# Moving the end of one stage and the start of the next: the slot maximum, the first logits loads and the last tile's activation

## The reference, cut to what matters

```python
logits = jnp.einsum('bnd,esd->bnes', x, phi)
dispatch = jax.nn.softmax(logits, axis=1)                      # over the nodes
combine = jax.nn.softmax(logits.reshape(B, N, E * S), axis=-1) # over all 4096 slots
slots = jnp.einsum('bnd,bnes->besd', x, dispatch)
h = jax.nn.gelu(jnp.einsum('besd,edh->besh', slots, w1) + b1[None, :, None, :])
y = jnp.einsum('besh,ehd->besd', h, w2) + b2[None, :, None, :]
out = jnp.einsum('besd,bnes->bnd', y, combine)
```

## Time and profile before

| what | us |
|---|---|
| median of three runs | 1797.23 (1797.04 to 1797.39) |
| the profiled execution's own time | 1797.73 |
| its span, first to last instruction | 1795.9 |
| mean granted clock of TensorE, share of full | 0.972 |
| TensorE busy in the span | 1620.2 |
| VectorE busy | 1103.3 |
| ScalarE busy | 848.6 |

### The profile page before, as it was taken

The page is one execution under the profiler, slowest core; times in us unless marked ns, Lnnn a source line. Parts: engine busy times, 40 slices in busy tenths (PEclk is TensorE's granted clock), DMA queues, the critical chain, the costliest instruction groups (busy, mean ns, idle before and its releaser), DMA issues. The chain is left out here.

```text
span 1795.9 us, 27185 instructions
## 1 busy us (share of the span) xinstructions
PE 1620.2 (90%) x9543; PEld 952.1 (53%) x9543; DVE 1103.3 (61%) x1844; ACT 848.6 (47%) x1306; POOL 267.8 (15%) x123
## 2 busy tenths in 40 slices
PE   6886664899999899899998999999999959998998
PEld 3433332565665566455544666655556536665555
DVE  7999997799999554532222555555555555665301
ACT  2269997888888454211112333333333335555100
POOL 0000001788788141000000000000000000000000
PEclk9999988799999999999999999999999989999999
DMA  4001000012222320311102211222222134441111
GB/s 171 18 28 49 23 23 1 26 34 33 34 48 20 81 77 1 124 36 36 36 9 73 69 59 57 69 69 69 69 69 69 60 127 139 151 150 39 64 53 51
DMA packets 49203, 108.38 MB, mean 60 GB/s; under 512 B 16222, under 2 KB 18232, under 8 KB 48988
## 3 DMA queue, kind: packets, MB, share of 16 engines
q1 hardware_dynamic: 49052, 107.18, 19.4%
q10 hardware_dynamic: 64, 0.08, 0.0%
HBM read 78.82 MB, written 28.43 MB: 60 GB/s over the span
## 5 line engine op out<-in xcount | busy, mean ns | idle before, releaser
L987 POOL TENSOR_TENSOR base<-s_row,ln_c 128x1250 f32<-128x1250 f32 x80 | 227.6, 2847 | 54.4 <-DVE top L1049 52.1
L99 PE MATMUL di_l<-x2t_hi,ph_hi 128*128 128x512 f16 (+1 forms) x576 | 195.5, 339 | 5.2 <-POOL p L1629 3.8
L100 PE MATMUL di_l<-x2t_lo,ph_hi 128*128 128x512 f16 (+1 forms) x576 | 195.5, 339 | 0.0
L101 PE MATMUL di_l<-x2t_hi,ph_lo 128*128 128x512 f16 (+1 forms) x576 | 195.5, 339 | 0.0
L1136 PE MATMUL at_o<-pt,h 128*128 128x384 f32 (+1 forms) x480 | 186.5, 526 | 0.0
L882 PE MATMUL fs<-one_src,one_dst 128*128 128x512 f16 x720 | 117.7, 318 | 66.4 <-ACT one_dst L793 54.3
L1115 PE MATMUL at_t<-ident,q 128*128 128x128 f32 x800 | 108.5, 285 | 31.4 <-ACT q L1021 30.7
L1688 DVE SCALAR_TENSOR_TENSOR pt_lo<-di_t,pt_hi 128x1280 f16<-128x1280 f32 x32 | 47.7, 1492 | 140.5 <-ACT pt_hi L1642 140.5
L628 DVE TENSOR_SCALAR one_src<-iota,src,worth 128x625 f16<-128x625 f16 x360 | 132.0, 444 | 3.3 <-PE fs L882 2.3
L99 PE MATMUL co_c<-ps_hi,hid_hi 128*128 128x305 f16 (+1 forms) x384 | 115.3, 300 | 20.4 <-DVE ps_lo L1931 20.1
L1115 PEld LDWEIGHTS at_t<-ident,q 128*128 128x128 f32 x800 | 93.1, 146 | 76.0 <-ACT q L1021 66.9
(11 more groups left out here) (276 smaller groups left out, 3311.0 us busy)
## 6 DMA issues: line engine op xcount, KB each, us to landing
logits_t<-lg SPq DMA_DIRECT2D x32, 625.0 KB, 3.6
logits_in<-logits_t SPq DMA_DIRECT2D x32, 625.0 KB, 4.6
phf<-in_phi SPq DMA_DIRECT2D x32, 384.0 KB, 3.9
w2f<-in_w2t SPq DMA_DIRECT2D x16, 384.0 KB, 3.6
s_row<-a_rows SPq DMA_DIRECT2D x9, 640.0 KB, 6.1
ew1f<-in_fw SPq DMA_DIRECT2D x6, 768.0 KB, 5.1
wf<-in_fw SPq DMA_DIRECT2D x12, 384.0 KB, 5.1
xs<-in_x SPq DMA_DIRECT2D x10, 384.0 KB, 4.6
```

Source lines behind the costliest of these rows:

```text
L99: eng.matmul(out, lh, rh, start=first, stop=False, skip_group_check=True)
L100: eng.matmul(out, lh, rl, start=False, stop=False, skip_group_check=True)
L101: return eng.matmul(out, ll, rh, start=False, stop=last, skip_group_check=True)
L987: eng.tensor_tensor(base[:, k % 2, 0:N], s_row[:, head % 2, 0:N], ln_c[:, j, 0:N], ALU.add)\
```

## The change

It has three parts.

First, the maximum. VectorE's ten reductions over 128 columns become one over a view of ten times 128 columns. It stands ahead of the activation of tile 30 in step 32. TensorE's last transpose moves from the end of step 32 into the middle of the 30 products, ahead of node tile 5, and ScalarE's copy `top_row` stands ahead of the tanh of tile 30.

Second, the loads. The buffer `logits_in` is laid out before `dispatch` (over the memory of `x2t`, which is read last by the logits of tile 31), and SyncE issues the first two loads of `combine` at the end of its step loop in `dispatch`, once the last logits are computed and the tiles 0 to 3 are stored. The wait for `slots_top` leaves SyncE and becomes VectorE's first wait in `combine`.

Third, the last tile. Of tile 31's activation only `g` is left in `dispatch`. Its other seven instructions are issued in `combine`: three on VectorE after step 1 of group 0, the tanh after ScalarE's step 2, `twice` after VectorE's step 2, the high half after ScalarE's step 3, and the low half in VectorE's group 1. TensorE waits for it ahead of group 2, and SyncE ahead of the weight loads of group 2.

```diff
@@ dispatch, SyncE
             run(eng, step)
+            eng.wait_ge(l_done, ST)
+            for u in range(2):
+                eng.wait_ge(kept[u], 16 * (EARLY_LOADS * 2 // 2))
+            for i in range(EARLY_LOADS):
+                eng.dma_start(logits_in[:, i, :, :], logits[2 * i:2 * i + 2, :, 0:HALF]
+                              .rearrange("s p n -> p s n")).then_inc(in_logits[i], 16)
             eng.wait_ge(max_row, 1)
...
-            eng.wait_ge(in_top, 16)
@@ dispatch, ScalarE: moved ahead of the tanh from the end of the step
+                if logits_end(s):
+                    eng.wait_ge(max_turned2, 1)
+                    eng.activation(top_row[:, :], lp[0:NT, NP:NP + P], ACT.Copy, bias=-math.log(S_PROB))\
+                       .then_inc(max_row, 1)
-                if valid(s - 2):
+                if here(s - 2):
@@ dispatch, VectorE
+                if logits_end(s):
+                    eng.wait_ge(max_turned, 1)
+                    eng.tensor_reduce(top_col[:, :], lp[:, 0:NP].rearrange("p (t n) -> p t n", t=NT),
+                                      AX_X, ALU.max).then_inc(max_col, 1)
...
-                    for t in range(NT):
-                        eng.tensor_reduce(top_col[:, t:t + 1], lp[:, t * P:(t + 1) * P], AX_X, ALU.max)\
-                           .then_inc(max_col, 1)
-            eng.wait_ge(hid_lo, ST)
+            eng.wait_ge(hid_lo, ST - 1)
+            eng.wait_ge(gel, 4 * (ST - 1) + 1)
@@ dispatch, TensorE, inside the products of tile 31
                     for t in range(NT):
+                        if logits_end(s) and t == NT // 2:
+                            eng.wait_ge(max_col, 1)
+                            eng.transpose(lp[0:NT, NP:NP + P], top_col[:, :], const["ident"][:, :])\
+                               .then_inc(max_turned2, 1)
@@ combine, SyncE
-            load(0, 0, 0)
-                for i in range(1, STEPS):
+                for i in range(EARLY_LOADS if G == 0 else 1, STEPS):
+                if G == 2:
+                    eng.wait_ge(hid_lo, ST)
@@ combine, ScalarE, after the high half of a step
+                if isinstance(G, int) and G == 0 and i == 2:
+                    eng.wait_ge(gel, 4 * ST)
+                    eng.activation(th[:, :], g2[:, :], ACT.Tanh, scale=0.7978845608028654).then_inc(th_ready, 1)
+                if isinstance(G, int) and G == 0 and i == 3:
+                    eng.wait_ge(twice, ST)
+                    eng.activation(hid[0][:, ST - 1, :], g1[:, :], ACT.Copy, scale=S_ACT / 2).then_inc(hid_hi, 1)
@@ combine, VectorE
+            eng.wait_ge(last["in_top"], 16)
             subtract(0, 0)
             step(0, 0, 0)
             for G in range(GROUPS):
                 for i in range(1, STEPS):
                     step(G, G % 2, i)
+                    if G == 0 and i == 1:
+                        last_inputs()
+                    if G == 0 and i == 2:
+                        last_twice()
+                    if G == 1 and i == 1:
+                        last_low()
```

More of the change, by code:

```diff
@@ L70 @@
 THIRD = 418
+EARLY_LOADS = 2
 DST_CHUNKS = ((0, 4), (4, 3), (7, 3))
@@ L210, in build @@
     after_top = mem.at
-    dispatch(nc, mem, sem, const, x2t, xw, phi, fb1, running_max, hid, scratch["logits"], slots_top,
-             scratch["row_max"], phf, ph, after_phi, in_phi, ph_hi, ph_lo)
     mem.at = base
@@ L215, in build @@
     end_comb = mem.at
-    assert end_comb <= temps
+    assert end_comb == after_xw
+    logits_in = mem("logits_in", [P, STE // 2, 2, HALF], F32)
+    after_logits = mem.at
+    assert after_logits <= temps
+    in_logits = [sem(f"co_in{i}") for i in range(STE // 2)]
+    mem.at = after_top
+    last = dispatch(nc, mem, sem, const, x2t, xw, phi, fb1, running_max, hid, scratch["logits"], slots_top,
+                    scratch["row_max"], phf, ph, after_phi, in_phi, ph_hi, ph_lo, logits_in, in_logits)
     mem.at = after_top
@@ L219, in build @@
     after_sums = mem.at
-    mem.at = end_comb
-    logits_in = mem("logits_in", [P, STE // 2, 2, HALF], F32)
+    mem.at = after_logits
     wf2 = [mem(f"wf2_{k}", [P, D], F32) for k in range((end_running - mem.at) // (D * 4))]
@@ L229, in build @@
     wf2 = combine(nc, mem, sem, slots_top, hid, comb, slot_sums, logits_in, scratch["logits"], wf2, late_at, fw2,
-                  in_w2)
+                  in_w2, in_logits, last)
     mem.at = end_running
@@ L1554, in dispatch @@
 def dispatch(nc, mem, sem, const, x2t, xw, phi, fb1, running_max, hid, logits, slots_top, max_rows,
-             phf, ph, after_phi, in_phi, ph_hi, ph_lo):
+             phf, ph, after_phi, in_phi, ph_hi, ph_lo, logits_in, in_logits):
     lg = mem("lg", [P, 2, N], F32)
@@ L1592, in valid, with here @@
             return not isinstance(s, int) or 0 <= s < ST
+        def here(s):
+            return valid(s) and not (isinstance(s, int) and s == ST - 1)
         def run(eng, step):
@@ L1672, in step @@
                                    accum_out=den[:, u:u + 1]).then_inc(p_ready, 1)
[L1673 to L1676, removed]
             run(eng, step)
@@ L1739, in step @@
                                       ALU.mult).then_inc(inv_ready, 1)
-                if logits_end(s):
-                    eng.wait_ge(max_turned, 1)
-                    for t in range(NT):
-                        eng.tensor_reduce(top_col[:, t:t + 1], lp[:, t * P:(t + 1) * P], AX_X, ALU.max)\
-                           .then_inc(max_col, 1)
             run(eng, step)
             eng.wait_ge(max_ready, ST)
-            eng.wait_ge(hid_lo, ST)
+            eng.wait_ge(hid_lo, ST - 1)
+            eng.wait_ge(gel, 4 * (ST - 1) + 1)
         @block.tensor
@@ L1791, in step, with combine @@
                     mm.then_inc(h_done, 1)
[L1792 to L1795, removed]
             run(eng, step)
-def combine(nc, mem, sem, top, hid, comb, slot_sums, lt, logits, wf, late_at, fw2, in_w):
+    return {"g": g, "g1": g1, "g2": g2, "th": th, "gel": gel, "th_ready": th_ready, "twice": twice,
+            "hid_hi": hid_hi, "hid_lo": hid_lo, "in_top": in_top}
+def combine(nc, mem, sem, top, hid, comb, slot_sums, lt, logits, wf, late_at, fw2, in_w, in_l, last):
     STEPS = STE // 2
@@ L1813, in combine @@
     sums_dram = nc.dram_tensor("slot_sums", [EXPERTS * STRIPS, N], F32).ap()
-    in_l = [sem(f"co_in{i}") for i in range(STEPS)]
+    g, g1, g2, th = (last[n] for n in ("g", "g1", "g2", "th"))
+    gel, th_ready, twice, hid_hi, hid_lo = (last[n] for n in ("gel", "th_ready", "twice", "hid_hi", "hid_lo"))
     sub_ready, p_ready, hi_ready, lo_ready, ones_ready = (
@@ L1943, in finish, with last_inputs, last_twice, last_low @@
                                              ALU.mult, ALU.subtract).then_inc(c_lo, 1)
+            def last_inputs():
+                k = ST - 1
+                eng.wait_ge(gel, 4 * k + 1)
+                eng.tensor_tensor(g1[:, :], g[:, :], g[:, :], ALU.mult).then_inc(gel, 1)
+                eng.wait_ge(gel, 4 * k + 2)
+                eng.tensor_scalar(g1[:, :], g1[:, :], 0.044715, 1.0, ALU.mult, ALU.add).then_inc(gel, 1)
+                eng.wait_ge(gel, 4 * k + 3)
+                eng.tensor_tensor(g2[:, :], g1[:, :], g[:, :], ALU.mult).then_inc(gel, 1)
+            def last_twice():
+                eng.wait_ge(th_ready, ST)
+                eng.scalar_tensor_tensor(g1[:, :], th[:, :], 1.0, g[:, :], ALU.add, ALU.mult).then_inc(twice, 1)
+            def last_low():
+                eng.wait_ge(hid_hi, ST)
+                eng.scalar_tensor_tensor(hid[1][:, ST - 1, :], g1[:, :], S_ACT / 2, hid[0][:, ST - 1, :],
+                                         ALU.mult, ALU.subtract).then_inc(hid_lo, 1)
+            eng.wait_ge(last["in_top"], 16)
             subtract(0, 0)
```

## The result

| | before | after |
|---|---|---|
| median of the runs, us | 1797.04 (7 runs, 1795.88 to 1797.39) | 1788.64 (7 runs, 1786.49 to 1793.98) |
| ratio, 95% interval | | 0.9957 [0.9948, 0.9967] |
| profiled execution: its time / span | 1797.73 / 1795.9 | 1793.74 / 1792.0 |

The account below looks back on a forecast made before the run. TensorE was taken as the bound, with a 15.4 us hole between dispatch and combine. The terms -8.7 + 0 + 0 + 0 on the median 1797.23 gave 1788.5 us, range 1786.5 to 1791.3.

Parts of the forecast that it names:

- The maximum: VectorE, end of dispatch: one reduction takes 1.49 us, no added TensorE wait; slots_top lands at 1460.57, not 1464.51.
- The loads: SyncE, end of dispatch: two loads issued at about 1445.9 and 1446.3, down by about 1452 to 1454, costing nothing.
- The end of the block: End of dispatch: combine begins 0.8 to 1.0 us before slots_top lands; first subtraction at about 1460.6, 8.7 us gained.
- The last tile: Seven instructions moved into combine: all covered, costing nothing; 3.9 us if no cover held.
- Rival C: In combine, the moved instructions are on the path after all: 3.9 us back, time 1792.4; chance 0.05.
- GpSimd's fillings: Start of combine, beside VectorE's first subtraction: cost taken as zero, upper bound 1.1 us.
- The clock: TensorE's hole before combine: clock still falls; low time costs 2.6 and 2.3 us as before, 1 us either way.
- Rival A: Start of combine: the stage opens more slowly than thought, by 1 to 3 us, time 1790.5; chance 0.11.
- B: End of dispatch: early loads do not come early (held or slow); 5.3 us gained, time 1791.9; chance 0.04.
- D: First groups of combine: holes in TensorE's work keep the clock low; slower than before, 1800.5; chance 0.02.

Follow-up runs that it names:

- the repeat: The changed kernel run again unchanged, on another chip: median 1787.63 us, ratio to before 0.9953 [0.9941, 0.9966].

## Why the prediction was right, step by step

*The maximum.* The reduction took 1.48 us (1.49 taken from `pt_lo`), the transpose came 4.00 us behind the landmark (3.99 expected) without a wait, and cost TensorE 0.11 us. From it to the read's issue there were 1.84 us (1.87 expected). The landing took 3.8 us and not 3.4. That is the one term that was mis-sized: `slots_top` at 9.7 and not 9.3, so 8.3 us of gain at this point and not 8.7. What makes it vary no run shows. In thirteen of the fourteen traces it took 3.4 to 4.0 us, in one 4.6.

*The loads.* Issued from 1450.64 on, both had landed by 1458.1, 2.4 us before the row's write at 1460.54 (more than 2 us of cover expected); they were never waited for, and four of them changed nothing.

*The end of the block.* VectorE's tail ended 8.03 us behind the landmark (8.0 expected). The step into `combine` took 0.60 us, longer than both rows that I had (0.28 and 0.51), so the stage opened 8.63 us behind the landmark, 1.0 us ahead of the landing at 9.64. With the landing of 3.4 us that I had forecast it would have been 0.6 us. The kernel without the last tile shows the price when it is not ahead: 2.9 us.

*The last tile.* Covered, as its rows above show. The kernel without it has the same F - S, and its stretch of `combine` differs by the clock's d / 2 alone. Rival C is refuted.

*GpSimd's fillings.* They ran from 1464.57 to 1466.5, across the start of the subtraction at 1465.61. The 32 subtractions took 1.453 to 1.462 us, as before. In the kernel without the last tile all of the fillings but their first 0.1 us (1468.48 to 1470.4) ran beside the first two subtractions, which took 2.83 us from 1468.59 on, as they do without fillings beside them (1477.14 in the kernel before). So the trace agrees with the Trainium skill's "SBUF — State Buffer" (section "SBUF: two separate sides"), by which a filling, which reads nothing, does not hold up an operation with two SBUF inputs; the shorter wording of the Trainium skill's "GPSIMD Engine Reference" (section "Specifications") would have it otherwise.

*The clock.* It fell as expected. The low times after the two restarts were 4.8 and 4.3 us (1656.10 to 1660.4) against 5.2 and 4.6, which gave 0.3 us back. So the two misses, 0.4 lost and 0.3 won, nearly cancel: 8.6 us from the landmark to the end, for 8.7 forecast. That part of the agreement is luck. So is the 0.1 us between the forecast and the median: the changed kernel's seven runs lie from 1786.49 to 1793.98, and the three in the middle alone span 2.0 us. On the chip of the repeat the medians differ by 8.6 us.

Rival A did not show (the stage opened ahead of the landing), nor B (the loads were early), nor D (the clock rose after 4.8 us, with TensorE dense). What I had not foreseen is that the changed kernel's runs spread over 7.5 us; in the two profiles that I compared, most of the difference is a wait upstream of the change.

## What to carry to other kernels

At a boundary between stages, write down every chain that the first instruction of the new stage waits for, with its end: here the row's round trip, the last engine's tail, and the first load. Shortening one chain gains only down to the next, so price the parts together; alone they gave 1.4, 4.4 and nothing, and together 8.3. A hole in TensorE's work of 8 to 16 us cost another 1.6 to 2.7 us after its end here, which matmuls of no use give back; fill the hole at the next boundary too: with the first one alone filled, the price of the next was 0.6 us higher.

## What the runs showed of the hardware

- Holes of 7.8 to 15.7 us on TensorE lowered the clock from 2.4 to 1.2 GHz; d us from the restart to the rise cost d / 2, to 0.1 us in twelve traces, with d from 3.1 to 5.4.
- A broadcast read of 640 KB behind a write of 5 KB took 3.4 to 4.0 us to land, and 4.6 in the one kernel where two loads of 625 KB were issued 1.2 us behind it. One case: that the loads delayed it is likely, not shown.
- The step from one stage to the next took 0.57 to 0.60 us where VectorE was last.
- Two executions of the same kernel differed by 6.6 us, 5.4 of it in waits for one kind of load in another stage (one landing took 10.9 us and not 4.7); a landmark inside the changed stage makes differences of 0.1 us readable in single profiles.
